# Chunk 0 of the MLP projected and normalised inside attention's last 40 steps, weighing in pairs to the end, and the eighth key tile of the last halves summed on TensorE

## The reference, cut to what matters

```
h = modulate(rmsnorm(x, g1, D), scale_msa, shift_msa)
q, k, v = split(h @ Wqkv.T + bqkv)                  # 16 heads of 32
q = rmsnorm(q, gq, hd) * hd ** (-0.5); k = rmsnorm(k, gk, hd)
attn = softmax(einsum('bhqd,bhkd->bhqk', q, k))
o = einsum('bhqk,bhkd->bhqd', attn, v)
x = x + gate_msa * (o @ Wproj.T + bproj)
h = modulate(rmsnorm(x, g2, D), scale_mlp, shift_mlp)
h = gelu(h @ Wfc1.T + bfc1, approximate=True)
x = x + gate_mlp * (h @ Wfc2.T + bfc2)
```

## Time and profile before

| | us |
|---|---|
| median of three runs | 1812.02 (1808.69 to 1813.46) |
| the profiled execution | 1810.62 |
| its span, first to last instruction | 1808.8 |
| attention, first exponential to last weighing | 69.6 to 978.3 |
| from the last attention weighing to the first lift | 978.3 to 1000.0 |
| the eight chunks | 1000 to 1809 |

### The profile page before, as it was taken

The page is one execution under the profiler, slowest core; times in us unless marked ns, Lnnn a source line. Parts: engine busy times, 40 slices in busy tenths (PEclk is TensorE's granted clock), DMA queues, the critical chain, the costliest instruction groups (busy, mean ns, idle before and its releaser), DMA issues.

```text
span 1808.8 us, 23247 instructions
## 1 busy us (share of the span) xinstructions
PE 1727.9 (96%) x8376; PEld 1154.5 (64%) x8376; DVE 1085.6 (60%) x1325; ACT 919.6 (51%) x1136; POOL 372.5 (21%) x305
## 2 busy tenths in 40 slices
PE   6998999999999999999889999999999999999998
PEld 3554555555555555554224787878788887878786
DVE  6678888898898898878788545142332324142301
ACT  4476666777777777778787432222221212221221
POOL 3001111100001000000140233333332333333332
PEclk8999999999999999999999899999999999999999
DMA  5754545555555555555765201010020202010000
GB/s 195 214 144 132 135 123 139 132 147 135 154 135 134 146 130 156 127 135 153 174 144 196 74 18 58 25 52 24 12 70 6 64 17 64 17 52 23 17 18 24
DMA packets 122242, 176.92 MB, mean 98 GB/s; under 512 B 29568, under 2 KB 43904, under 8 KB 121136
## 3 DMA queue, kind: packets, MB, share of 16 engines
q1 hardware_dynamic: 115952, 156.41, 32.3%
q10 hardware_dynamic: 5408, 16.81, 2.5%
q0 software_dynamic: 800, 2.62, 0.5%
HBM read 124.87 MB, written 50.92 MB: 97 GB/s over the span
## 4 chain that ended last, share of the span: by engine, by line
PE 44%; issue 29%; DVE 11%; POOL 9%; ACT 4%; DMA 2%; SPq 0%; POOLq 0%; ACTq 0%; DVEq 0%
PE scores L513 9%; PE pv L530 8%; PE gemm L588 7%; DVE sums L791 5%; PE scores L1303 5%; POOL act_parts L1235 5%; PE gemm L601 4%; ACT probs L704 3%; PE pv L1320 3%; PE gemm L1320 2%; PE aux L554 2%; POOL y L1233 2%; PE aux L547 1%; DVE raw L816 1%; DVE raw L862 1%
## 5 line engine op out<-in xcount | busy, mean ns | idle before, releaser
L704 ACT ACTIVATE probs<-scores,shift 128x1024 f32<-128x1024 f32 x512 | 548.7, 1113 | 195.4 <-PE scores L513 178.7
L791 DVE TENSOR_TENSOR sums<-sums,probs 128x2048 f32<-128x2048 f32 x192 | 453.8, 2363 | 32.7 <-ACT probs L704 28.0
L513 PE MATMUL scores<-q_stack,k_stack 128*128 128x512 f32 x1024 | 358.8, 435 | 6.3 <-ACT probs L704 6.1
L1303 PE MATMUL scores<-w_hi,act_parts 128*128 128x512 f32 x1024 | 318.7, 392 | 0.0
L513 PEld LDWEIGHTS scores<-q_stack,k_stack 128*128 128x128 f32 x1024 | 173.8, 189 | 202.3 <-issue 105.5
L1235 POOL TENSOR_TENSOR act_parts<-act_full,act_parts 128x512 fp32r<-128x512 f32 x128 | 172.5, 1348 | 514.2 <-ACT act_parts L1166 513.6
L530 PE MATMUL pv<-probs,v 128*32 128x512 f32 x2048 | 253.1, 603 | 0.4 <-ACT probs L704 0.4
L1303 PEld LDWEIGHTS scores<-w_hi,act_parts 128*128 128x128 f32 x1024 | 191.4, 189 | 38.8
L1303 PE MATMUL scores<-w_lo,act_parts 128*128 128x512 f32 x512 | 199.9, 391 | 0.0
L1373 DVE TENSOR_TENSOR y_next<-pv,p_bias 128x512 f32<-128x512 f32 x28 | 19.3, 691 | 299.7 <-PE pv L1275 299.7
L1166 ACT ACTIVATE act_parts<-act_full 128x512 fp32r<-128x512 f32 x128 | 80.9, 632 | 224.5 <-PE scores L1303 223.5
(11 more groups left out here) (167 smaller groups left out, 1944.1 us busy)
## 6 DMA issues: line engine op xcount, KB each, us to landing
k_stack<-parts_scratch SPq DMA_DIRECT2D x128, 256.0 KB, 5.0
q_stack<-parts_scratch SPq DMA_DIRECT2D x128, 256.0 KB, 5.1
parts_scratch<-parts SPq DMA_DIRECT2D x62, 512.0 KB, 2.9
inverse<-inverse_scratch SPq DMA_DIRECT2D x128, 64.0 KB, 2.1
heads_out<-o_out SPq DMA_DIRECT2D x32, 256.0 KB, 5.2
out<-result SPq DMA_DIRECT2D x32, 256.0 KB, 2.0
heads<-heads_out SPq DMA_DIRECT2D x28, 256.0 KB, 3.6
x_tile<-in_x SPq DMA_DIRECT2D x28, 256.0 KB, 2.8
```

The costliest lines, as they stand in the source:

```text
L513: mm = nc.tensor.matmul(scores[p][:, i, :], k_stack[s][:, h, j * P:(j + 1) * P], q_stack[half][:, h, :], start=True, stop=True)
L704: nc.scalar.activation(probs[L % RING][:, 2 * p:2 * p + 2, :], scores[p][:], ACT.Exp, bias=small["shift"][:]).then_inc(exp_done, 1)
L791: nc.vector.tensor_tensor(sums[:], a[:], probs[l % RING][:], ALU.add).then_inc(added, 1)
L1303: mm = nc.tensor.matmul(acc[t], act_parts[m % 2][:, b, t * P:(t + 1) * P], w2[a][:, m, :], start=(m == 0 and i == 0), stop=(m == NM - 1 an ...
```

## The change

Five things change together. (1) `PAIRED = AFTER`: steps 208 to 255 weigh in pairs too. (2) The projection of chunk 0 is cut into single matmuls and put between the scores of steps 222 to 249, seven steps for each tile of 128 tokens, two matmuls in each of a tile's first five steps and one in the last two. All four tiles use one bank (`gemm`), so tile t waits until VectorE has moved tile t - 1 out (`proj_moved`). Gating, the square sum, clamp, inverse root and normalisation of tile t follow 0 to 3 steps behind its last matmul; the normalised tiles go to buffers of their own in place of w1's second half. (3) The heads are loaded from step 213, in consecutive steps, and split from step 219 on. (4) From half 26 on VectorE adds six tiles; TensorE sums `sums` and then the eighth tile's `probs` into the same bank, and the exponential that reuses this buffer waits for it. (5) Behind attention only transposes and z remain: ScalarE makes tiles 1 and 3, VectorE tiles 0 and 2; the copy of the last row sums, gelu's table and the weights from w1(2) on come behind that. `LEAN` is 26, `TAIL` 213.

```diff
+LEAN = -(-max(FILL) // NT)
+def adds_until(l):
+    hh, j = l // NT, l % NT
+    return ADDS * min(hh, LEAN) + (ADDS - 1) * max(0, hh - LEAN) + (min(j, ADDS - 1) if hh >= LEAN else j)
...
-PAIRED = max(FILL)
-HEADS_LOAD, BIAS_LOAD, X_LOAD = {TAIL + 2 + 3 * t: t for t in range(CT)}, TAIL + 14, {TAIL + 17 + 3 * t: t for t in range(CT)}
-HEADS_HIGH, HEADS_LOW, X_BIASED = ({TAIL + after + 2 * t: t for t in range(CT)} for after in (18, 19, 34))
+PAIRED = AFTER
+PROJ_STEPS = 7
+PROJECT = {TAIL + 9 + PROJ_STEPS * t + i: (t, i) for t in range(CT) for i in range(PROJ_STEPS)}
+HEADS_LOAD, BIAS_LOAD, X_LOAD = {TAIL + t: t for t in range(CT)}, TAIL + 5, {TAIL + 6 + t: t for t in range(CT)}
+HEADS_HIGH, HEADS_LOW = ({TAIL + after + 3 * t: t for t in range(CT)} for after in (6, 7))
+X_BIASED = {TAIL + 11 + 3 * t: t for t in range(CT)}
+PROJ_OUT, PROJ_SQUARE, PROJ_CLAMP, PROJ_NORM = ({TAIL + 9 + PROJ_STEPS * (t + 1) + after: t for t in range(CT)} for after in range(4))
...
-            pe.wait_ge(added, ADDS * (hh + 1))
+            pe.wait_ge(added, adds_until(NT * hh + NT - 1))
-                mm = nc.tensor.matmul(aux[h * DH:(h + 1) * DH, :], small["ones"][:], sums[:, h, :], start=True, stop=True)
+                mm = nc.tensor.matmul(aux[h * DH:(h + 1) * DH, :], small["ones"][:], sums[:, h, :], start=True, stop=(hh < LEAN))
+            if hh >= LEAN:
+                l = NT * hh + NT - 1
+                pe.wait_ge(exp_done, 2 * l + 2)
+                for h in range(HG):
+                    mm = nc.tensor.matmul(aux[h * DH:(h + 1) * DH, :], small["ones"][:], probs[l % RING][:, h, :], start=False, stop=True)
...
             if L >= 0:
                 qk(L, 0)
             fill(L, 0)
+            mlp_step(L, 0)
             if L >= 0:
                 qk(L, 1)
             if L in ROWS_AT and L > PAIRED:
...
-                act.wait_ge(added, ADDS * (l // NT) + max(1, l % NT))
+                act.wait_ge(added, adds_until(l + 1 if l % NT == 0 else l))
+                if l // NT >= LEAN and l % NT == NT - 1:
+                    act.wait_ge(rs_mm, l // NT + 1)
...
-            if j == 0:
+            if j == 0 or hh >= LEAN and j == NT - 1:
-                dve.wait_ge(added, hh * ADDS + j - 1)
+                dve.wait_ge(added, adds_until(l - 1))
...
-                load_w2(i)
-                if i + 1 < NM // LOADED:
-                    load_w1(i + 1)
-            move_rows()
-            square(0)
-            square(1)
-            high1(2)
+            load_w2(0)
+            load_w1(1)
+            load_w2(1)
             act.wait_ge(pv_mm, AFTER)
-            square(2)
+            first_z(1)
             turn_tile(0, 0)
-            square(3)
             turn_tile(0, 1)
-            act.preload_act_table(ACT.Gelu_apprx_tanh)
+            first_z(3)
             turn_tile(0, 2)
             turn_tile(0, 3)
+            move_rows()
+            act.preload_act_table(ACT.Gelu_apprx_tanh)
+            high1(2)
             high2(0)
             high2(1)
             act.wait_ge(f1_in, 16)
+            act.wait_ge(z_lo, CT)
+            load_w1(2)
+            load_w2(2)
+            load_w1(3)
...
+            if L in PROJ_CLAMP:
+                inverse_root(PROJ_CLAMP[L])
-            for t in range(CT - 1):
-                inverse_root(t)
-            inverse_root(CT - 1)
...
     def tensor(pe):
         pairs = ((0, 0), (0, 1), (1, 0))
-        def first_projection(t):
+        def step(L, part):
+            if L not in PROJECT:
+                return
+            t, i = PROJECT[L]
+            terms = [(k, a, b) for k in range(KT) for a, b in pairs]
+            counts = [2] * (len(terms) - PROJ_STEPS) + [1] * (2 * PROJ_STEPS - len(terms))
+            lo = sum(counts[:i]) + part
             r = slice(t * P, (t + 1) * P)
-            pe.wait_ge(heads_lo, t + 1)
-            if t == 0:
-                pe.wait_ge(wp_low, KT)
-            for k in range(KT):
-                for i, (a, b) in enumerate(pairs):
-                    mm = nc.tensor.matmul(acc[t], z[b][:, k, r], wp[a][:, k, :], start=(k == 0 and i == 0), stop=(k == KT - 1 and i == 2))
-            mm.then_inc(proj_mm, 1)
+            if part >= counts[i]:
+                return
+            if lo == 0:
+                pe.wait_ge(heads_lo, t + 1)
+                if t == 0:
+                    pe.wait_ge(wp_low, KT)
+                    pe.wait_ge(raw_done, len(UNIT))
+                else:
+                    pe.wait_ge(proj_moved, t)
+            k, a, b = terms[lo]
+            mm = nc.tensor.matmul(up[0], z[b][:, k, r], wp[a][:, k, :], start=(lo == 0), stop=(lo == len(terms) - 1))
+            if lo == len(terms) - 1:
+                mm.then_inc(proj_mm, 1)
         def last(row_sums):
-            first_projection(0)
+            for t in range(CT):
+                turn_tile(0, t)
             row_sums()
-            first_projection(1)
-            first_projection(2)
-            turn_tile(0, 0)
-            first_projection(3)
-            for t in range(1, CT):
-                turn_tile(0, t)
...
+                if isinstance(c, int) and c == 0:
+                    pe.wait_ge(proj_moved, CT)
+            if m == 1 and isinstance(c, int) and c == 0:
+                pe.wait_ge(o_done, NC * NG - 1)
...
+            if L in PROJ_OUT:
+                first_y(PROJ_OUT[L])
+            if L in PROJ_CLAMP:
+                first_clamp(PROJ_CLAMP[L])
+            if L in PROJ_NORM:
+                first_norm(PROJ_NORM[L])
...
-            if t >= 2:
-                dve.wait_ge(y_stat, t - 1)
-            nc.vector.tensor_tensor(result[t % 2][:], acc[t], gate1[:], ALU.mult).then_inc(proj_moved, 1)
+            dve.wait_ge(x_biased, t + 1)
+            if t == 0:
+                dve.wait_ge(gate1_first_in, 16)
+            nc.vector.tensor_tensor(first[t], up[0], gate1[:], ALU.mult).then_inc(proj_moved, 1)
-            nc.vector.tensor_tensor(y_next[:, t, :], y_next[:, t, :], result[t % 2][:], ALU.add).then_inc(y_done, 1)
+            nc.vector.tensor_tensor(y_next[:, t, :], y_next[:, t, :], first[t], ALU.add).then_inc(y_done, 1)
...
-            dve.wait_ge(mod_ready, 1)
-            dve.wait_ge(pv_mm, AFTER - 1)
-            first_y(0)
-            first_clamp(0)
-            first_norm(0)
-            first_y(1)
-            first_clamp(1)
-            dve.wait_ge(rs_mm, NC * NG)
-            first_y(2)
-            first_norm(1)
-            first_clamp(2)
             first_z(0)
-            first_y(3)
-            first_norm(2)
+            first_z(2)
             first_z_low(0)
-            first_z(1)
-            first_clamp(3)
             first_z_low(1)
-            first_norm(3)
-            first_z(2)
-            first_z(3)
             first_z_low(2)
             first_z_low(3)
+            low1(1)
             low1(2)
             invert()
             output()
...
+    put_all("z_full_first", a + 48 * K, CT, [KT, P])
+    put_all("y_norm_first", a + 56 * K, CT, [D])
```

More of the change, by code:

```diff
@@ L492, in tensor @@
     def tensor(pe):
-        mlp_last = mlp["tensor"](pe)
+        mlp_step, mlp_last = mlp["tensor"](pe)
         issued = dict(squares=0, turns=0, rows=0)
@@ L626, in tensor @@
             fill(L, 1)
+            mlp_step(L, 1)
             if L in SUM_AT:
@@ L935, in build_mlp @@
     gated = result[0][:]
+    first = [y[:, t, :] for t in range(CT)]
     scores, pv = psum["scores"], psum["pv"]
@@ L973, in turn_bank, with normed_y, full_z @@
         if isinstance(c, int) and c == 0:
-            return acc[t] if k < KT // 2 else (up + acc)[t]
+            return acc[t]
         return turn
+    def normed_y(c, t):
+        return mem["y_norm_first"][t] if isinstance(c, int) and c == 0 else y_norm[t % 2]
+    def full_z(c, t):
+        return mem["z_full_first"][t] if isinstance(c, int) and c == 0 else z_full[t % 2]
     def norms_before(c):
@@ L1092, in step @@
                 nc.scalar.activation(z[0][:, :, t * P:(t + 1) * P], heads_first[t], ACT.Copy).then_inc(heads_hi, 1)
+            if L in PROJ_SQUARE:
+                square(PROJ_SQUARE[L])
             if L in W1_LOAD:
@@ L1119, in last @@
             act.wait_ge(f1_in, 16)
+            act.wait_ge(z_lo, CT)
+            load_w1(2)
+            load_w2(2)
+            load_w1(3)
+            load_w2(3)
             chunks(nothing, turn_tile, mlp, nothing, act.Fori)
@@ L1124, in square, with first_z @@
             act.wait_ge(y_done, t + 1)
-            if t == 0:
-                act.wait_ge(pv_mm, AFTER - 1)
-            nc.scalar.activation(result[t % 2][:], y_next[:, t, :], ACT.Square, accum_out=y_sq[:, t:t + 1]).then_inc(y_stat, 1)
+            nc.scalar.activation(first[t], y_next[:, t, :], ACT.Square, accum_out=y_sq[:, t:t + 1]).then_inc(y_stat, 1)
+        def first_z(t):
+            act.wait_ge(turned, t + 1)
+            act.wait_ge(mod_ready, 1)
+            for k in range(KT):
```

(48 more changed lines are left out.)

12 lines of the change are left out of this document (2 added, 10 removed).

## The result

The changed kernel took 1839.18 us (median of four runs, 1835.38 to 1839.93), the kernel before, run beside it, 1811.03 (1808.69 to 1813.46, four runs): ratio 1.0150, 95% interval 1.0138 to 1.0162. The forecast was 1832 in a range of 1816 to 1846. The profiled spans differ by as much as the medians, 1837.0 - 1808.8 = 28.2 us, so the account can be made in the traces. The mechanism was as forecast; the sum was 8 us short (20.0 against 28.2).

A forecast was written before the change was run, and what follows sets the result against it. The prediction took the loop between three almost full engines (TensorE, ScalarE, VectorE) as the bound. Its terms, 14.7 + 8.1 + 3.2 + 4.8 - 13.8 + 3.0 = +20.0 us, gave 1832 us, range 1816 to 1846.

The forecast's parts named there:

- Parts 1 to 3: Step 209's row sums to the last pair: paired weighings, extra row sums and projection matmuls lengthen the loop, +14.7 us.
- Part 4: Steps 229, 236 and 243: TensorE waits for VectorE to empty the one projection bank, +8.1 us.
- The lengthening by GpSimd: At the three bank hand-overs: GpSimd lockout lengthens VectorE's adds, 0.9 us each, 2.7 in all, left out of the sum.
- Part 5: Step 219: exponentials wait for the copy of chunk 0's last head load, +3.2 us (0 to 5).
- Part 6: Behind the heads' stall and those at steps 229 and 243: TensorE's clock drops, +4.8 us (0 to 8).
- Part 7: Behind attention: the way from the last pair to the first lift matmul shrinks to 10.4 us, -13.8 us.
- Part 8: Lift to down(0): the last half's inverse, with its memory trips, holds up VectorE's queue, +3 us (0 to 5).
- the clock gate: Rival, chance 0.08: a third of the 23 paired cycles run at half clock, +20 us, 1852 us.
- faster: Rival, chance 0.10: the second weighing hides, two steps stay at 4.69 us, -7.5 us, 1804 us.
- Even exchange: Rival, chance 0.13: heads land in time, VectorE is ahead at hand-overs, clock holds; only +4 us, 1816 us.

The follow-up runs named there:

- e3: The changed kernel with two projection matmuls in each of six steps and a seventh step free between tiles: 1824.45 us, ratio 1.0077 to the kernel before.
- e1: The kernel before with one edit, steps 208 to 255 weighing in pairs: 1822.34 us, ratio 1.0055.
- e10: e7 with the MLP's eight 1 MB weight loads spread one by one: 1805.11 us, ratio 0.9971 to the kernel before.
- e6: The kernel before, single weighings, with TensorE instead of VectorE summing the eighth key tile's probabilities from half 26 on: 1802.63 us, ratio 0.9969.
- e7: The changed kernel with single weighings, a free seventh step, heads split three steps later and the last four weight loads at tile 2: 1825.71 us, ratio 1.0094.
- e9: The changed kernel with the MLP's eight 1 MB weight loads spread one by one: 1833.94 us, ratio 1.0133 to the kernel before.
- e5: The changed kernel with the last four weight loads issued behind the third gelu instead of ahead of the first: 1841.1 us, ratio 1.0174 to the kernel before.

## Why the prediction was nearly right, and where it was short

From the row sums of step 209 to the last pair 160.1 us passed (851.24 to 1011.37), before 124.8: +35.3. With the start 0.2 later, -14.4 and +7.1 behind, that is the 28.2.

- **Parts 1 to 3**, +14.7: right. Cycles of 5.54 us, 5.77 with a projection matmul in the loop, 7.26 with two groups of row sums; put together from such cycles, without stalls and slow clock, the stretch has 139.2 us, +14.4.
- **Part 4**, +8.1: right, 8.7 us of waits, some 8.3 of it added. Removed by e3. The lengthening by GpSimd was rightly left out of the sum. At the first hand-over the add of 918.03 took its 2.29 us with GpSimd beside it; it was GpSimd's instruction, begun 0.56 us later, that took 2.86 instead of 1.28. By the Trainium skill ("SBUF — State Buffer", section "SBUF: two separate sides") the instruction that starts first keeps the shared ports for its whole length and the other one is blocked; the trace agrees here. At the other two hand-overs (948.29 and 972.25) GpSimd was not at work.
- **Part 5**, +3.2: right in kind, 5.6. The load was issued 1.1 us later than before and took 6.4, above the 6.1 of my upper end, and the exponential stood for the whole copy.
- **Part 6**, +4.8: about 7.0, which is what the other terms leave of the 35.3. I had three times 1.6. Cycle by cycle it is about 1.8 behind the heads, 2.5 to 2.8 behind each stall of 3.29 us, and next to nothing behind the one of 2.17. The pairs behind the stalls took 3.24 to 3.61 us instead of 1.92. That the price is higher than at the earlier trace rows because a whole pair and projection matmuls now stand in the loop behind a stall is likely, but no run isolates it.
- **Part 7**, -13.8: right, -14.4; from last pair to lift 9.74 us, forecast 10.4.
- **Part 8**, +3: this is the term that was mis-sized most. It measured +7.1, outside its own ends of 0 and 5. From the lift to down(0) I had 13.6 us and it took 17.3. The first two trips, for which I took 5.9 of a range of 3 to 8, lasted 9.1 (row store 1020.76 to reciprocal 1029.84), and the way back 7.2 instead of 6.3. The trace of before already had the price: under the weight loads the store took 4.8, as I wrote, but the read of the compact rows behind it (issued at 987.83) took another 7.2 to land, where 1.7 is the median over that kernel. I priced one of the two trips. Before, this was hidden: the weights were all issued by 980, and VectorE came for the rows only at 1000.50, when they lay ready and the way back was free of loads. Now four of the loads were issued with the very trips, and VectorE waited for them.

Terms too low by 2.4, 2.2 and 4.1 make the 8 us. That the forecast range held 1839 is in part luck. The ends that Parts 5, 6 and 8 state add up to 9.0 and 27.0 us, 1821 to 1839; the 1844 of the forecast's "own range" doesn't follow from them, and the measured 28.2 lies above them. The margin covered it, not the terms.

Of the rivals, the clock gate did not come: in the changed kernel the paired cycles away from stalls ran at full clock (16 matmuls in 1.92 us) with 1.1 us idle in each 5.5. But e1 shows that this is not safe: one of its 23 cycles fell to half clock with no stall ahead of it (961.38). I had taken from the Trainium skill ("TensorE: Matmul & The Clock Gate", section "HAM oscillation — how this bites in real kernels") that this rival would be the likely one. But the kernel of that section waits for a DMA in every tile, longer than the tile's matmuls take; the paired cycle here is not of that kind, so the section did not make the rival likely. The rival "faster" fell with the first cycle. "Even exchange" is true of the projection by itself, for another reason than I gave: e10 against e6.

The hoped-for gain thus went four ways: into pairs that add to the loop (+10 alone), into short stalls (the heads and three hand-overs), three of them with a slow clock behind, into weights that cross the last inverse, and, what I had not seen, into TensorE itself, which had hardly any free time there.

## What to carry to other kernels

Before work is moved into a stretch, read the busy share of its engine there, and without the stalls that the change itself removes: the earlier trace rows has 90% with the stalls of the row sums in it, e6 has 96% without them. At 96% the move is an exchange, and only the waits that it removes behind are a gain. When small transfers run beside large ones, price each of them from a row, not the first alone. When a stage becomes shorter, look at what transfers start at its end and what small trips they now meet, since a load of a few MB that is free at one place costs 7 to 10 us at another. And split a change into its parts: one part of this one gained 6 us by itself, while the whole lost 28.

## What the runs showed of the hardware

Small trips through memory suffer from large loads issued beside them from another engine's queue. Four reads of 64 KB took 9.0 us from the first issue to use beside three loads of 1 MB (e7), 3.4 and 3.3 with none beside them (e9 and e10, the last inverse). A read of 8 KB took 7.4 us beside four such loads and 1.7 without (changed kernel and e9). The issue of a 256 KB load stood 8.13 us behind four loads (e5), 1.19 without (e9). Spreading the same loads took 20.6 us from a kernel. Which resource they share (the rings, the engines or the memory) stays open.

TensorE's granted clock fell to 0.50, the 1.2 GHz level, behind stalls of 3.10 to 6.34 us in attention of the kernels before and after, and not behind one of 2.17; in e1 it also fell behind one of 1.76 and once behind a pause of 1.10. The length of the last stall alone does not tell whether it falls.
